# A third panel in flight: four P and PT buffers instead of three, in the attention of a transformer layer

## The chip, the cores and the metric

The kernel runs on the 8 cores of one Trainium2 chip, four on each of its two dies. Every core executes the same program on its own inputs, and no core waits for another. The time is the device time of the slowest core in microseconds, as the median of several runs. The profile is of one execution, read on its slowest core.

## What is computed

One layer on x of 4 sequences x 4096 positions x 2048 features: causal attention with 16 heads of 128, a low-rank key and value path (latent 512), rotary embedding, and then a gated feed-forward with int8 weights (8192 wide), each inside "norm, block, norm, add":

```python
def attn(x):                                  # x is layer-normed
    q = x @ Wq + bq
    kv = x @ Wdown
    k, v = kv @ Wk_up, kv @ Wv_up             # 16 heads of 128
    q, k = rope(q), rope(k)
    scores = einsum('bhqd,bhkd->bhqk', q, k) / sqrt(128)
    scores = where(causal, -10000.0, scores)
    ctx = einsum('bhqk,bhkd->bhqd', softmax(scores), v)
    return ctx @ Wo + bo
def ffn(x):
    return ((silu(x @ w_gate * s_gate) * (x @ w_up * s_up)) @ w_down) * s_down
x = x + layernorm(attn(layernorm(x)))
x = x + layernorm(ffn(layernorm(x)))
```

## The kernel before

Two cores share a sequence. Each computes keys and values for all 4096 positions and takes 16 of the 32 blocks of 128 queries, so chosen that block number tt (0 to 15) of either core sees at most 256 (tt + 1) keys: `wpad(tt)` is that width W.

The program is written as a plan. `plan.step(engine, fn, waits)` appends one step to the list of an engine (T is TensorE, V VectorE, S ScalarE, G GpSimd, Q the SP queue, SyncE), and each engine executes its list strictly in the order of appending. A `Slot` stands for a buffer: `cons_waits` waits for whoever filled it, `prod_waits` also for its last readers. DMAs of one queue share 8 semaphores in turn. There are five stages, A to E, with a barrier over all engines behind each. A makes keys and values, B the queries, C is the attention proper, D the output projection with norm and first sum, E the feed-forward.

Stage C is the one that matters here. It loops over 16 heads h, and within a head over 16 tiles tt. One head and one tile are a panel. For a panel:

- TensorE multiplies the 128 queries with up to 512 keys at a time (L706) into one of four PSUM banks, chunk ci into bank ci. There are 1 to 8 chunks. VectorE adds the causal mask to the last 256 columns (L720) and takes the negated maximum of the first chunk (L728). ScalarE takes the exponential of each chunk with that maximum as bias (L734), writes P in bf16 and accumulates the row sums in `lacc`.
- VectorE adds the row sums (L746) and takes the reciprocal (L750).
- The SP queue issues one DMA transpose of the whole panel from `P_b[par]` to `PT_b[par]` (L756), within SBUF.
- `emit_ctx` multiplies PT with V, W / 128 matmuls of 128 columns (L667), into bank 4 or 5, and VectorE scales the result by the reciprocal into `ctx` (L678).

The context of a panel is not appended in its own iteration. Panels are put in the list `pend`, and `emit_ctx` is called for the oldest when there are more than two. So behind the scores of tile tt stands the context of tile tt - 2, and behind those of tiles 0 and 1 the contexts of tiles 14 and 15 of the head before. On VectorE the eviction of that context stands ahead of the maximum of the next tile. P, PT, `lacc`, `lsum`, `negc` and `rl_s` have three buffers, taken in turn (`par`).

K, V and Q of the next head are loaded by `head_loads(h + 1)` ahead of tile 4: K (L640) and Q (L650) from ScalarE's queue, V as a DMA transpose from HBM (L645) on the SP queue. These have two buffers each. The lines of the core of this:

```python
                pend.append((par, hp, W, tt, h))
                if len(pend) > 2:
                    emit_ctx(pend.pop(0))
        while pend:
            emit_ctx(pend.pop(0))
```

Of the kernel before, what the change touches and what calls it, by code (L numbers as in the profile page):

```python
# [8 lines left out]
BF16 = mybir.dt.bfloat16  # L9
# [120 lines left out]
def build_program():  # L130
# [91 lines left out]
    sg_s = small([64])  # L222
    su_s = small([64])
    st_s = small([16])
    lacc = small([24])
    lsum = small([3])
    negc = small([3])
    rl_s = small([3])
    assert sm_off[0] <= 512

    ps = [e(nc.psum_tensor(f"ps{i}", [128, 512], F32)) for i in range(8)]
# [384 lines left out]
    if "C" in PHASES:  # L616
        ccv = Carver(arena, AR_U)
        k_s = [ccv.take([SEQ], BF16) for _ in range(2)]
        v_t = [ccv.take([32, 128], BF16) for _ in range(2)]
        q_s = [ccv.take([TOK], BF16) for _ in range(2)]  # L620
        P_b = [ccv.take([SEQ], BF16) for _ in range(3)]
        PT_b = [ccv.take([32, 128], BF16) for _ in range(3)]
        mks_s = ccv.take([NH, 256], F32)
        ctx = ar_view(ctxr, 0, [NH, DM], BF16)

        s_k = [Slot(), Slot()]
        s_v = [Slot(), Slot()]
        s_q = [Slot(), Slot()]
        s_P = [Slot(), Slot(), Slot()]
        s_PT = [Slot(), Slot(), Slot()]  # L630
        s_m = Slot()
        s_ctx = Slot()
        s_lac = [Slot(), Slot(), Slot()]
        s_rl = [Slot(), Slot(), Slot()]

        s_m.produced(st("Q", lambda q: q.dma_start(mks_s, mks), dma="dQ"))

        def head_loads(h):
            hp = h % 2
            ev = st("S", lambda s, h=h, hp=hp: s.dma_start(  # L640
                k_s[hp], k_scr[h * 128:(h + 1) * 128, :]),
                waits=prod_waits(s_k[hp]) + cons_waits(scr_slot["k"]),
                dma="dA")
            s_k[hp].produced(ev)
            ev = st("Q", lambda s, h=h, hp=hp: s.dma_start(  # L645
                v_t[hp], v_scr[h * 128:(h + 1) * 128, :], transpose=True),
                waits=prod_waits(s_v[hp]) + cons_waits(scr_slot["v"]),
                dma="dQ", xpose=True)
            s_v[hp].produced(ev)
            ev = st("S", lambda s, h=h, hp=hp: s.dma_start(  # L650
                q_s[hp], q_scr[h * 128:(h + 1) * 128, :]),
                waits=prod_waits(s_q[hp]) + cons_waits(scr_slot["q"]),
                dma="dA")
            s_q[hp].produced(ev)

        head_loads(0)
        pend = []

        def emit_ctx(p):
            (par, hp, W, tt, h) = p  # L660
            cbank = 4 + (len(pend) + h + tt) % 2
            cps, cpa = ps_slot[cbank], ps_ap[cbank]

            def fn(t, par=par, hp=hp, W=W, cpa=cpa):
                r = None
                for kc in range(W // 128):
                    r = t.matmul(cpa[:, 0:128], PT_b[par][:, kc, :],  # L667
                                 v_t[hp][:, kc, :],
                                 start=(kc == 0), stop=(kc == W // 128 - 1))
                return r  # L670
            ev_c = st("T", fn, waits=prod_waits(cps) +
                      cons_waits(s_PT[par], s_v[hp]))
            cps.produced(ev_c)
            s_PT[par].used(ev_c)
            s_v[hp].used(ev_c)

            ev_e = st("V", lambda v, tt=tt, h=h, par=par, cpa=cpa:
                      v.tensor_scalar(ctx[:, tt, h * 128:(h + 1) * 128],  # L678
                                      cpa[:, 0:128],
                                      rl_s[:, par:par + 1], None,  # L680
                                      op0=ALU.mult),
                      waits=cons_waits(cps, s_rl[par]))
            cps.used(ev_e)
            s_rl[par].used(ev_e)
            s_ctx.produced(ev_e)

        pancnt = 0
        for h in range(NH):
            hp = h % 2

            for tt in range(16):
                if tt == 4 and h + 1 < NH:
                    head_loads(h + 1)
                par = pancnt % 3
                pancnt += 1
                W = wpad(tt)
                nch = (W + 511) // 512
                exp_evs = []
                ev_nc = None
                for ci in range(nch):  # L700
                    n0 = ci * 512
                    N = min(512, W - n0)
                    bank = (ci + pancnt * 4) % 4
                    pss, psa = ps_slot[bank], ps_ap[bank]
                    ev_mm = st("T", lambda t, tt=tt, hp=hp, n0=n0, N=N, psa=psa:
                               t.matmul(psa[:, 0:N],  # L706
                                        q_s[hp][:, tt * 128:(tt + 1) * 128],
                                        k_s[hp][:, n0:n0 + N],
                                        start=True, stop=True),
                               waits=prod_waits(pss) +  # L710
                               cons_waits(s_q[hp], s_k[hp]))
                    pss.produced(ev_mm)
                    s_q[hp].used(ev_mm)
                    s_k[hp].used(ev_mm)
                    ev_ready = ev_mm
                    if ci == nch - 1:
                        moff = (W - 256) - n0
                        assert moff >= 0
                        ev_ready = st("V", lambda v, psa=psa, moff=moff, tt=tt:
                                      v.tensor_add(psa[:, moff:moff + 256],  # L720
                                                   psa[:, moff:moff + 256],
                                                   mks_s[:, tt, :]),
                                      waits=[ev_mm] + cons_waits(s_m))
                        pss.produced(ev_ready)
                    if ci == 0:
                        N0 = N
                        ev_nc = st("V", lambda v, psa=psa, N0=N0, par=par:
                                   v.reduce_max(negc[:, par:par + 1],  # L728
                                                psa[:, 0:N0],
                                                axis=AX, negate=True),  # L730
                                   waits=[ev_ready] + prod_waits(s_lac[par]))
                        pss.used(ev_nc)
                    ev = st("S", lambda s, psa=psa, n0=n0, N=N, par=par, ci=ci:
                            s.activation(P_b[par][:, n0:n0 + N], psa[:, 0:N],  # L734
                                         ACT.Exp, bias=negc[:, par:par + 1],
                                         scale=1.0,
                                         accum_out=lacc[:, par * 8 + ci:
                                                        par * 8 + ci + 1]),
                            waits=[ev_ready, ev_nc] +
                            (prod_waits(s_P[par]) if ci == 0 else []))  # L740
                    pss.used(ev)
                    exp_evs.append(ev)
                s_P[par].produced(exp_evs[-1])
                s_lac[par].produced(exp_evs[-1])

                ev_l = st("V", lambda v, par=par, nch=nch: v.reduce_sum(  # L746
                    lsum[:, par:par + 1], lacc[:, par * 8:par * 8 + nch],
                    axis=AX),
                    waits=exp_evs)
                ev_rl = st("V", lambda v, par=par: v.reciprocal(  # L750
                    rl_s[:, par:par + 1], lsum[:, par:par + 1]),
                    waits=[ev_l] + prod_waits(s_rl[par]))
                s_rl[par].produced(ev_rl)
                s_lac[par].used(ev_l)

                ev_t = st("Q", lambda q, par=par, W=W: q.dma_start(  # L756
                    PT_b[par][:, 0:W // 128, :], P_b[par][:, 0:W],
                    transpose=True),
                    waits=cons_waits(s_P[par]) + prod_waits(s_PT[par]),
                    dma="dQ", xpose=True)  # L760
                s_P[par].used(ev_t)
                s_PT[par].produced(ev_t)

                pend.append((par, hp, W, tt, h))
                if len(pend) > 2:
                    emit_ctx(pend.pop(0))

        while pend:
            emit_ctx(pend.pop(0))

        plan.barrier()
# [478 lines left out]
```

How the kernel before makes its waits and increments, by code:

```python
    def replay(self, eng_handle, eng_name, sems):  # L85
        cur = {}
        for ws, fn, sem, inc in self.ops[eng_name]:
            for s, v in ws:
                if cur.get(s, 0) < v:
                    eng_handle.wait_ge(sems[s], v)
                    cur[s] = v
            if fn is None:
                continue
            inst = fn(eng_handle)
            if inc:
                inst.then_inc(sems[sem], inc)
```

## Time and profile before

| | |
|---|---|
| median of 3 runs | 6945.17 us (6869.4 to 7135.95) |
| profiled execution | 6705.15 us |
| its span, slowest core (core 3) | 6703.6 us |
| spans of the 8 cores | 6675.4 to 6703.6 us |
| granted clock, mean of a core | 0.837 to 0.842 |
| busy, share of the span | PE 66%, DVE 25%, ACT 19%, POOL 12% |

The span is from the first to the last instruction of a core. The profiled execution is 1.5 us longer than its span, and 3.5% below the median of the three runs. PE is TensorE (PEld its weight loads), DVE VectorE, ACT ScalarE, POOL GpSimd, SP the queue of SyncE. The granted clock is a share of 2.4 GHz, so 0.50 is the level of 1.2 GHz and 1.00 that of 2.4. In a timeline row stand the start (us from the start of the span), the duration, engine, line, operation, output and input, and in brackets how long the engine sat idle ahead of it and what ended that.

### The profile page before, as it was taken

Reading aid. Unit: us, or ns where it says so; the run is one execution under the profiler, and the core shown is the slowest. Engines: PE = TensorE matmul, PEld = TensorE weight load, DVE = VectorE, ACT = ScalarE, POOL = GpSimd, SP = SyncE. Lnnn points to the kernel's source line nnn. Section 1 sums busy time; section 2 is a strip of 40 time slices with the busy share of each in tenths; the row PEclk is TensorE's granted clock in tenths of the full one; section 3 lists DMA queues with packets and bytes.
Section 4 is the critical chain, followed back from the end, with each engine's and each line's share of the span. In section 5 each row is a group of like instructions: output and inputs, shape, how many; then the busy total and the mean of one; then the engine's idle time right before and its main releaser. Section 6 shows DMA issues by size and latency. Waiting matters only on the chain.

```text
span 6703.6 us, 67697 instructions; the slowest of 8 cores (6675.4 to 6703.6 us)
## 1 busy us (share of the span) xinstructions
PE 4411.7 (66%) x21376; PEld 2030.9 (30%) x21376; DVE 1656.0 (25%) x3157; ACT 1283.3 (19%) x3035; POOL 780.1 (12%) x732
## 2 busy tenths in 40 slices
PE   0334443366566665663333899879998899879986
PEld 0111111133333333341111344334433344334432
DVE  0333433244333333332333111021101211021101
ACT  0111111011555555550111000010000110010100
POOL 0111211133000000000000111111111111111111
PEclk9867776688777777766666999989999999999998
DMA  9333233522777777765443999489967898489954
GB/s 183 96 94 91 75 107 94 129 58 64 140 138 138 139 138 137 138 125 144 129 138 108 165 153 155 128 166 153 151 140 153 152 154 139 128 168 154 153 125 132
DMA packets 1566328, 883.21 MB, mean 132 GB/s; under 512 B 777122, under 2 KB 1541026, under 8 KB 1550242
## 3 DMA queue, kind: packets, MB, share of 16 engines
q0 software_dynamic: 679296, 434.14, 38.0%
q1 hardware_dynamic: 839842, 327.28, 22.0%
q10 hardware_dynamic: 46848, 117.45, 5.2%
q8 instruction: 187, 3.06, 0.2%
q14 instruction: 155, 1.27, 0.1%
HBM read 398.53 MB, written 109.05 MB: 76 GB/s over the span
## 4 chain that ended last, share of the span: by engine, by line
PE 45%; DMA 21%; DVE 11%; ACT 8%; issue 8%; SPq 3%; POOL 2%; another core or an unknown queue 1%; ACTq 0%; DVEq 0%; POOLq 0%
PE ps L994 13%; PE ps L1008 13%; PE ps L1061 7%; DMA arena<-wd 7%; ACT arena L734 5%; PE ps L826 3%; DMA arena<-arena 3%; DMA ctxr<-xin 3%; PE ps L667 2%; PE ps L706 2%; PE ps L395 2%; PE ps L426 2%; POOL arena L589 1%; DMA ctxr<-x_scr 1%; DVE smalls L728 1%
## 5 line engine op out<-in xcount | busy, mean ns | idle before, releaser
L994 PE MATMUL ps<-arena 128*128 128x512 bf16 x4096 | 933.2, 381 | 228.0 <-DMA arena<-x1n_scr 124.4
L1061 PE MATMUL ps<-arena 128*128 128x512 bf16 x4096 | 919.5, 380 | 140.3 <-DMA arena<-wd 138.4
L1008 PE MATMUL ps<-arena 128*128 128x512 bf16 x4096 | 925.8, 379 | 0.6 <-DMA arena<-wu 0.6
L734 ACT ACTIVATE arena<-ps,smalls 128x512 bf16<-128x512 f32 (+1 forms) x1152 | 748.6, 667 | 566.7 <-DVE smalls L728 366.4
L706 PE MATMUL ps<-arena 128*128 128x512 bf16 (+1 forms) x1152 | 473.8, 485 | 376.4 <-ACT arena L734 310.7
L994 PEld LDWEIGHTS ps<-arena 128*128 128x128 bf16 x4096 | 402.1, 98 | 718.5 <-issue 241.4
L395 PE MATMUL ps<-arena 128*128 128x512 bf16 x512 | 128.0, 417 | 722.8 <-DMA arena<-ctxr 722.8
L1061 PEld LDWEIGHTS ps<-arena 128*128 128x128 bf16 x4096 | 385.9, 98 | 673.3 <-issue 245.2
L1024 DVE TENSOR_SCALAR ctxr<-ps,smalls 128x512 bf16<-128x512 f32 x256 | 192.1, 750 | 1450.7 <-PE ps L1008 1450.4
L1008 PEld LDWEIGHTS ps<-arena 128*128 128x128 bf16 x4096 | 400.5, 98 | 484.4 <-issue 1.5
L667 PE MATMUL ps<-arena 128*128 128x128 bf16 x4352 | 417.9, 273 | 170.9 <-DMA arena<-arena 165.1
L984 POOL DMA_DIRECT2D arena<-wg x128 | 146.4, 1143 | 3292.1 <-DMA x1n_scr<-arena 2028.9
L1019 ACT ACTIVATE ctxr<-ps,smalls 128x512 bf16<-128x512 f32 x256 | 175.9, 687 | 1545.3 <-PE ps L994 1543.1
L826 PE MATMUL ps<-arena 128*128 128x512 bf16 x1024 | 229.9, 389 | 333.1 <-DMA arena<-wo_scr 306.1
L667 PEld LDWEIGHTS ps<-arena 128*128 128x128 bf16 x4352 | 376.9, 126 | 231.6 <-issue 223.6
L426 PE MATMUL ps<-arena 128*128 128x512 bf16 x1024 | 295.3, 427 | 121.3 <-DVE arena L461 110.1
L555 PE MATMUL ps<-arena,ctxr 128*128 128x512 bf16 x1024 | 231.0, 390 | 151.2 <-DMA arena<-xnf_scr 151.2
L706 PEld LDWEIGHTS ps<-arena 128*128 128x128 bf16 x1152 | 124.1, 114 | 652.7 <-issue 645.3
L1050 POOL DMA_DIRECT2D arena<-wd x256 | 189.7, 741 | 939.4 <-PE ps L1061 916.1
L395 PEld LDWEIGHTS ps<-arena 128*128 128x128 bf16 x512 | 53.4, 105 | 796.9 <-issue 747.6
L1081 DVE TENSOR_TENSOR ctxr<-ps,ctxr 128x512 f32<-128x512 f32 x64 | 43.9, 691 | 1012.6 <-PE ps L1061 1012.5
L469 POOL TENSOR_TENSOR ctxr<-arena 128x512 bf16<-128x512 f32 x128 | 162.2, 1267 | 946.1 <-DVE arena L461 946.1
(73 smaller groups left out, 2613.6 us busy)
## 6 DMA issues: line engine op xcount, KB each, us to landing
arena<-wg POOLq DMA_DIRECT2D x128, 1024.0 KB, 7.0
arena<-wu POOLq DMA_DIRECT2D x128, 1024.0 KB, 7.1
arena<-wd POOLq DMA_DIRECT2D x256, 512.0 KB, 3.8
ctxr<-xin SPq DMA_DIRECT2D x32, 1024.0 KB, 5.8
arena<-wo_scr ACTq DMA_DIRECT2D x16, 2048.0 KB, 8.9
xnf_scr<-arena SPq DMA_DIRECT2D x16, 1024.0 KB, 7.1
k_scr<-ctxr SPq DMA_DIRECT2D x16, 1024.0 KB, 7.1
v_scr<-ctxr SPq DMA_DIRECT2D x16, 1024.0 KB, 7.8
```

Of the source, the lines that this page charges most:

```text
L395: r = t.matmul(psa, wdn_s[:, fc, lc * 128:(lc + 1) * 128], xnfm[:, fc, :], start=(fc == 0), stop=(fc == NH - 1))
L426: r = t.matmul(psa, wts[:, lc, fc * 128:(fc + 1) * 128], kvl[:, lc, :], start=(lc == 0), stop=(lc == 3))
L555: rr = t.matmul(psa, wq_s[:, fc, oc * 128:(oc + 1) * 128], xnfmB[:, fc, :], start=(fc == 0), stop=(fc == NH - 1))
L667: r = t.matmul(cpa[:, 0:128], PT_b[par][:, kc, :], v_t[hp][:, kc, :], start=(kc == 0), stop=(kc == W // 128 - 1))
L706: t.matmul(psa[:, 0:N], q_s[hp][:, tt * 128:(tt + 1) * 128], k_s[hp][:, n0:n0 + N], start=True, stop=True),
L734: s.activation(P_b[par][:, n0:n0 + N], psa[:, 0:N], ACT.Exp, bias=negc[:, par:par + 1], scale=1.0, accum_out=lacc[:, par * 8 + ci: par * 8 ...
L826: r = t.matmul(psa, ctxfm[tp][:, fc, j * 128:(j + 1) * 128], wo_s[wop][:, fc, :], start=(fc == 0), stop=(fc == NH - 1))
L994: rr = t.matmul(ga, wg_s[slp][:, fc, icw * 128:(icw + 1) * 128], x1nfm[:, fc, :], start=(fc == 0), stop=(fc == NH - 1))
L1008: rr = t.matmul(ua, wu_s[slp][:, fc, icw * 128:(icw + 1) * 128], x1nfm[:, fc, :], start=(fc == 0), stop=(fc == NH - 1))
L1024: ev2 = st("V", lambda v, ic=ic, ua=ua: v.tensor_scalar(u_sb, ua, su_s[:, ic:ic + 1], None, op0=ALU.mult), waits=cons_waits(ub) + prod_wai ...
L1050: return g.dma_start(wd_s[qp], sap)
L1061: rr = t.matmul(psa, f_b[:, quar * 4 + ic, j * 128:(j + 1) * 128], wd_s[qp][:, ic, :], start=(quar == 0 and ic == 0), stop=(quar == 15 and ...
```

## The change

A third panel is in flight. P, PT and the small vectors get a fourth buffer, `emit_ctx` is called when more than three panels are pending, and the loads of the next head stand ahead of tile 5 instead of tile 4.

```diff
-    lacc = small([24])
-    lsum = small([3])
-    negc = small([3])
-    rl_s = small([3])
+    lacc = small([32])
+    lsum = small([4])
+    negc = small([4])
+    rl_s = small([4])
...
-        P_b = [ccv.take([SEQ], BF16) for _ in range(3)]
-        PT_b = [ccv.take([32, 128], BF16) for _ in range(3)]
+        P_b = [ccv.take([SEQ], BF16) for _ in range(4)]
+        PT_b = [ccv.take([32, 128], BF16) for _ in range(4)]
...
-        s_P = [Slot(), Slot(), Slot()]
-        s_PT = [Slot(), Slot(), Slot()]
+        s_P = [Slot() for _ in range(4)]
+        s_PT = [Slot() for _ in range(4)]
...
-        s_lac = [Slot(), Slot(), Slot()]
-        s_rl = [Slot(), Slot(), Slot()]
+        s_lac = [Slot() for _ in range(4)]
+        s_rl = [Slot() for _ in range(4)]
...
-                if tt == 4 and h + 1 < NH:
+                if tt == 5 and h + 1 < NH:
                     head_loads(h + 1)
-                par = pancnt % 3
+                par = pancnt % 4
...
                 pend.append((par, hp, W, tt, h))
-                if len(pend) > 2:
+                if len(pend) > 3:
                     emit_ctx(pend.pop(0))
```

On TensorE, at the boundary from one head to the next, this stands in a row before (L706 are scores, L667 contexts; x30 and x32 are the contexts of tiles 14 and 15, the row of 128x256 alone is tile 0 of the next head):

```order
L667 MATMUL ps5<-arena 128x128 x28
L706 MATMUL ps0<-arena 128x256
L667 MATMUL ps4<-arena 128x128 x30
L706 MATMUL ps0<-arena 128x512
L667 MATMUL ps5<-arena 128x128 x32
L706 MATMUL ps0<-arena 128x512
L706 MATMUL ps1<-arena 128x256
L667 MATMUL ps5<-arena 128x128 x2
```

The context of tile 15 stands behind the scores of tile 1. On the same engine and at the same place it now reads:

```order
L706 MATMUL ps0<-arena 128x256
L667 MATMUL ps4<-arena 128x128 x28
L706 MATMUL ps0<-arena 128x512
L667 MATMUL ps5<-arena 128x128 x30
L706 MATMUL ps0<-arena 128x512
L706 MATMUL ps1<-arena 128x256
L667 MATMUL ps4<-arena 128x128 x32
L706 MATMUL ps0<-arena 128x512
L706 MATMUL ps1<-arena 128x512
L667 MATMUL ps4<-arena 128x128 x2
```

Every context has moved behind the scores of one more tile; that of tile 15 now stands behind those of tile 2. On the SP queue, at the loads of the next head, this is the order (128x8x128 is the transpose of tile 3, 128x10x128 that of tile 4), first before:

```order
L756 DMA_TRANSPOSE arena<-arena 128x8x128
L645 DMA_TRANSPOSE arena<-v_scr 128x32x128
L756 DMA_TRANSPOSE arena<-arena 128x10x128
L756 DMA_TRANSPOSE arena<-arena 128x12x128
```

and after the change:

```order
L756 DMA_TRANSPOSE arena<-arena 128x8x128
L756 DMA_TRANSPOSE arena<-arena 128x10x128
L645 DMA_TRANSPOSE arena<-v_scr 128x32x128
L756 DMA_TRANSPOSE arena<-arena 128x12x128
```

The transpose of V has moved behind the transpose of tile 4. K and Q move by the same tile on ScalarE's queue.

## Rows read from the trace of the kernel before

**Rows 1.** The page: span, and ScalarE's busy tenths in 40 equal slices.
```profile
span 6703.6 us, 67697 instructions; the slowest of 8 cores (6675.4 to 6703.6 us)
...
ACT  0111111011555555550111000010000110010100
```

**Rows 2.** Stretch of stage C: length, busy times, granted clock, DMA share, GB/s.
```profile
1664.00:3030.00 1366.00, 831.70 (x5504) 494.92 (x5504) 424.01 (x1280) 773.16 (x2305) 0.00 (x0) 0.71 0.71 138
```

**Rows 3.** Waits, 1676 to 3030 us: us in total, times, longest.
```profile
ACT arena L734 <- DVE smalls L728: 366.4, 173, 8.9
...
ACT arena L734 <- PE ps L706: 181.7, 79, 4.7
PE ps L667 <- DMA arena<-arena: 165.1, 49, 6.3
...
ACT arena L734 <- PE ps L667: 18.6, 3, 6.4
...
SPq L90 <- ACT arena L734: 495.9, 191, 6.9
```

**Rows 4.** Timeline of ScalarE, head 15: first exponentials of tiles 5 and 8.
```profile
2957.07 0.69 ACT L734 ACTIVATE arena<-ps,smalls 128x512 bf16<-128x512 f32 x1 [1.62 <-DVE smalls L728]
...
2969.41 0.69 ACT L734 ACTIVATE arena<-ps,smalls 128x512 bf16<-128x512 f32 x1 [1.62 <-DVE smalls L728]
```

**Rows 5.** Timeline of ScalarE, tile 2: heads 1 and 15, of 15.
```profile
1768.13 0.69 ACT L734 ACTIVATE arena<-ps,smalls 128x512 bf16<-128x512 f32 x1 [5.89 <-PE ps L667]
...
2947.64 0.69 ACT L734 ACTIVATE arena<-ps,smalls 128x512 bf16<-128x512 f32 x1 [5.47 <-DVE smalls L728]
```

**Rows 6.** Timeline, head 1: tiles 5, 6 and 8, and a context of tile 3.
```profile
1777.57 0.69 ACT L734 ACTIVATE arena<-ps,smalls 128x512 bf16<-128x512 f32 x1 [1.62 <-DVE smalls L728]
...
1780.40 1.01 PE L667 MATMUL ps<-arena 128*128 128x128 bf16 x8 [3.62 <-DMA arena<-arena]
1782.85 0.69 ACT L734 ACTIVATE arena<-ps,smalls 128x512 bf16<-128x512 f32 x1 [3.16 <-PE ps L706]
...
1792.78 0.69 ACT L734 ACTIVATE arena<-ps,smalls 128x512 bf16<-128x512 f32 x1 [1.62 <-DVE smalls L728]
```

**Rows 7.** Timeline from 1923 us: the boundary from head 2 to head 3.
```profile
1923.54 1.83 PE L667 MATMUL ps<-arena 128*128 128x128 bf16 x30
...
1924.19 5.28 SPq L756 DMA_TRANSPOSE arena<-arena  x1
...
1929.22 0.19 ACT L734 ACTIVATION_READ_ACCUMULATOR arena<-ps,smalls 128x1 f32 x1
...
1931.58 3.57 PE L667 MATMUL ps<-arena 128*128 128x128 bf16 x32 [4.58 <-DMA arena<-arena]
...
1936.58 0.69 ACT L734 ACTIVATE arena<-ps,smalls 128x512 bf16<-128x512 f32 x1 [7.17 <-DVE smalls L728]
...
1937.61 0.20 ACT L734 ACTIVATION_READ_ACCUMULATOR arena<-ps,smalls 128x1 f32 x1
...
1939.43 0.69 ACT L734 ACTIVATE arena<-ps,smalls 128x512 bf16<-128x512 f32 x1 [1.62 <-DVE smalls L728]
```

**Rows 8.** Stretches ahead of and behind that wait, columns as in rows 2.
```profile
1920.00:1924.00 4.00, 3.17 (x41) 2.48 (x42) 0.43 (x1) 4.00 (x12) 0.00 (x0) 1.00 0.80 150
...
1932.00:1936.00 4.00, 3.82 (x33) 3.16 (x31) 0.67 (x2) 0.00 (x0) 0.00 (x0) 0.50 0.16 33
```

**Rows 9.** Head 2: load of V, end of tile 4, landings in 1845:1940, then 1863:1868.
```profile
1858.19 7.89 SPq L645 DMA_TRANSPOSE arena<-v_scr  x1
...
1859.88 0.20 ACT L734 ACTIVATION_READ_ACCUMULATOR arena<-ps,smalls 128x1 f32 x1
...
DMA to landing us min/median/max: 2.3/4.5/8.3
...
DMA to landing us min/median/max: 3.6/3.8/4.0
```

**Rows 10.** Stretch behind the loads in head 2, columns as in rows 2.
```profile
1864.00:1868.00 4.00, 2.50 (x12) 1.28 (x12) 1.71 (x5) 0.77 (x3) 0.00 (x0) 0.50 1.27 286
```

## The prediction, made before the result

> **What bounds the kernel now.** I began with the page: the span of the slowest core and the slices in which ScalarE is busy to five tenths [rows 1]. These slices are the attention stage, the only one that the change touches. The stretch query gives its extent, 1664 to 3030 us, 1366 us of 6703.6, with the DMA engines busy to 0.71 and a granted clock of 0.71 on average [rows 2]. Stages end in barriers over all engines, and the cores do not talk to each other, so what this stage loses or gains reaches the end one to one.
>
> Then the waits of this stage [rows 3]. ScalarE sat idle 366.4 + 181.7 + 18.6 = 566.7 us ahead of its exponentials (L734). TensorE waited 165.1 us, in 49 waits, for DMA transposes ahead of the context matmuls (L667). The SP queue, which issues all transposes, waited 495.9 us for ScalarE. No engine is full, so the stage is bound by a chain that goes round once per panel (a panel is one head and one tile of 128 queries, "tile n" below, 256 of them).
>
> The timeline shows that chain. In a quiet panel, ScalarE is idle for 1.62 us between the last exponential of one tile and the first of the next: head 15, which loads nothing, has 1.62 at tiles 5, 6, 7 and 8 [rows 4]. In these 1.62 us VectorE does, in a row, the sum, the reciprocal, the context eviction and the maximum, and ScalarE needs that maximum. 256 x 1.62 = 415 us, which the change leaves alone. So 566.7 - 415 = 152 us is all that ScalarE waits over the bare round, and the most that a perfect pipeline of this form could give back: 2.3% of the span.
>
> Two places hold most of the 152. First, the head boundary. The gap ahead of tile 2 is 5.89 us in head 1 and 5.47 in head 15, the first and the last of 15 such rows, which sum to 99.9 us; less 15 x 1.62 that is 75.6 us [rows 5]. Second, the loads of the next head: ahead of tiles 5 to 7 the gaps of heads 0 to 14 sum to 40.2 us over 1.62 each, 2.7 us per load. In head 1 it is 15.21 us from the start of tile 5 to that of tile 8 (1777.57 to 1792.78), in head 15 it is 12.34 (2957.07 to 2969.41) [rows 4, 6].
>
> **The boundary, step by step** [rows 7]. The transpose of tile 15 of head 2 is issued from 1924.19 on, behind its last exponential, for 5.28 us, and TensorE starts on its context (32 matmuls) at 1931.58, after 4.58 us of idling. Meanwhile tiles 0 and 1 of head 3, one exponential each, are soon done (tile 1 by 1929.41), and tile 2 can't start: its maximum stands on VectorE behind the eviction of this context. The exponential of tile 2 starts at 1936.58, that is 5.00 us after the context began. Tile 3 follows at 1939.43, 2.85 us later.
>
> With a depth of three, the context of tile 15 stands behind the scores of tile 2. What stands ahead of tile 2 is the context of tile 14, whose transpose has long landed: it ran at 1923.54 without a wait. So tile 2 can start at 1929.41 + 1.62 = 1931.0 and, at its 1.23 us (1936.58 to 1937.81), works until 1932.3, while the transpose lands. The context of tile 15 starts at 1931.58 as before, since nothing in the change speeds its transpose. If its matmuls take 3.57 us again, tile 3 starts at 1931.58 + 5.00 = 1936.58 and not at 1939.43: 2.85 us gained, 43 us in 15 boundaries. All 15 gaps are long enough for that: the least is 5.40 us, 3.8 over the 1.62.
>
> How fast these 32 matmuls run sets the rest. The granted clock was 1.00 in 1920 to 1924 and 0.50, the 1.2 GHz level, in 1932 to 1936, after the idling [rows 8]. At the upper level 30 of them took 1.83 us [rows 7], so 32 would take 1.95, and tile 3 could start 1.6 us sooner: 4.5 us per boundary, or, capped where a gap has less than that to give, 64 us in all. TensorE's wait here shrinks from 4.58 us to about 1.3 (from the end of tile 2's scores, near 1930.3), so some boundaries should keep the clock. I take 51, between 43 and 64 and nearer to the row of 3.57. Bounds: 0, if the transpose lands later by as much as is gained, and 75.6, all of it. The Trainium skill (TensorE: Matmul & The Clock Gate, Part 1) calls the half-rate clock the default, which activity releases and idling brings back; by that rule the boundaries would give the 64 us. The trace agrees in so far as the level is the lower one behind the idling and the upper one ahead of it.
>
> Against it: 30 matmuls (tile 14) now stand between the scores of tile 1 and those of tile 2. At the lower level they take some 3.3 us from 1927.0 and end at 1930.3, where the bank is free at 1929.3: 1.0 us late, 15 us in all at worst. It costs nothing as long as tile 3 waits for the context of tile 15 anyway, which it does at the lower level. I take 0 and keep 15 as the bound below nothing.
>
> **The loads.** The load of V is a transpose too, and holds SP for 7.89 us [rows 9]; now it goes ahead of the transpose of tile 4, with K and Q beside it. Therefore the context of tile 3 waits 3.62 us in head 1 [rows 6], and that of tile 4 nearly as long. It moves behind the transpose of tile 4. In head 2, tile 4's transpose would be issued near 1860.2 (its exponentials end at 1860.08), V from about 1861.5 to 1869.4, tile 5's transpose at 1869.4, landed by 1873.4 (4.0 us, the longer of two there [rows 9]). The context of tile 5 is now due behind the scores of tile 8, not before 1875: in time by 1.6 us. That of tile 4, if its landing is as slow as the slowest in that head, 8.3 us [rows 9], lands at 1868.5 and is due at 1870. A further 2 us would be hidden, since a wait of 3.62 us on TensorE cost ScalarE only 3.16 - 1.62 = 1.54 [rows 6]. I take 38 of the 40.2 us; bounds 0 and 40.2. What hides it is the third panel in flight. Without that, moving the load by a tile would only move the wait, and the 38 us would be 0.
>
> The Trainium skill (Perfetto Trace Analysis, What "DMA-bound" means) names as a bound an issuing engine whose sequencer track is solid with DMA work. More buffers would then give nothing, which is the second rival below. Here SP waited for ScalarE for 495.9 of 1354 us [rows 3], so its track isn't solid.
>
> **The rest** costs nothing: the fourth P and PT buffer only follow the depth, and no wait of before is for one of them to come free; the drain behind the last head still waits for the transpose of its tile 15; the start of the stage is the same; instructions and bytes are the same in number.
>
> **The sum.** 51 + 38 = 89 us. The profiled execution took 6705.15 us around a span of 6703.6, so its like would take 6616, 1.3% less. The runs shown have a median of 6945.17 and a lowest of 6869.4, both well above the profiled one. The stage's waits are counted in absolute microseconds, so I take the same 89 off the median: 6856 us.
>
> **Rivals.**
> *The loads' waits only move.* T4's landing or V's hold on SP is longer beside wider transposes, and contexts 5 and 6 wait at tiles 8 and 9 instead. The DMA engines were full (a share of 1.27 from 1864 to 1868) behind the loads in head 2 [rows 10], and the margin is only 1.6 us; but 2 us more are hidden. Then 51 us is gained: 6894.
> *Nothing is gained.* SP or the DMA engines bind, and tile 15's transpose lands as much later as its context is due later. 495.9 us of SP's waiting speaks against. 6945.
> *Nearly all goes.* The clock stays high through the boundaries, and the smaller gaps (152 - 116 = 36 us) shrink, since each tile has two context matmuls fewer beside it. Then 130 to 150 us: 6805, and past 2% at the far end.
> *Slower.* The loads now meet the transposes of tiles 4 to 6, wider than 3 to 5, and the big contexts of tile 14 delay the scores of tile 2 at the lower clock. If the load's waits double (40 us more) and the boundary gives nothing but pays its 15 us, 55 us are lost: 7000. It decides when TensorE's waits for transposes rise above 165.1 us; nothing in the rows of before points there.
>
> **How the numbers follow.** The forecast has 0.65, moved waits 0.14, nothing 0.06, nearly all 0.10, slower 0.05. All cases together reach from 6805 to 7000, and the runs of before alone lie 1.1% below to 2.7% above their median, which the median of a few new runs inherits in part; so 6710 to 7000. 2% of the median, 139 us, is about what a measurement of this kernel can tell from no change. Only the far end of one case is beyond it by itself; with the spread of runs I give 0.18 to faster by over 2%, 0.78 to within 2%, and 0.04 to slower.
>
> **What would show it.** In the profile after: the stage some 89 us shorter than 1366; TensorE's wait for transposes ahead of L667 down from 165.1 us to under 40; the gap ahead of tile 2 near 1.6 to 2.6 us, and one of 2 to 4 us ahead of tile 3 in its place; tiles 6 and 7 at 1.62 as in head 15; everything outside the stage as before. Waits for transposes that appear ahead of tiles 8 and 9 would show the moved wait. The forecast is wrong if the gap ahead of tile 2 stays above 5 us, or if the gap at tile 3 takes its whole length.

## The result, and the profile after

| | before | after |
|---|---|---|
| median of 10 runs | 6891.2 us | 6692.67 us |
| lowest run | 6707.85 us | 6604.59 us |
| ratio, with 95% interval | | 0.9845 (0.9829 to 0.9861) |
| first to last exponential of stage C, mean of cores 4 to 7 | 1333.7 us | 1232.2 us |
| the same, mean of all 8 cores, after in the second measurement | 1333.9 us | 1234.1 us |

About half of the runs of either kernel were disturbed, with a lower clock on one die or both, and the three runs of before that were known ahead were all of that kind: the ratio is taken without such runs, while the medians hold both. The ratio is a gain of 1.55%, 104 us of the 6705 of the profiled execution (0.0155 x 6705). In a second measurement, with runs of the kernel before beside it, the ratio was 0.9863 (0.982 to 0.9905). The forecast was 89 us, 1.3%.

"The stage" is here the time from the first exponential of stage C to the last. In the trace of the first measurement cores 4 to 7 had nearly the same granted clock as before (0.841 to 0.844, against 0.839 to 0.842), and they are the ones read. There the stage of core 4 took 1333.6 us before and 1228.8 after (1686.9 to 2915.7), 105 us less; the mean of the four cores fell by 101.5 us, and in the second measurement the mean of all eight by 99.8. The profiled core of before, core 3, is the longest of its eight with 1337.7 us (1678.8 to 3016.6), so it can't be set against another core. The rest of the span of cores 4 to 7 was 9 us longer on average, 5363.9 us against 5354.8. The change does not touch it, and it differs by as much and more between single executions, as the part on depth alone shows.

The rows below are of the changed kernel in the second measurement, core 3, whose stage took 1237.9 us. First the page, and the stretch of the stage with the columns of [rows 2]:

```profile
span 6614.1 us, 67712 instructions; the slowest of 8 cores (6580.0 to 6614.1 us)
...
ACT  0111111111566666641111000010000100010000
```

```profile
1664.00:2930.00 1266.00, 837.78 (x5495) 481.47 (x5496) 415.04 (x1279) 772.21 (x2305) 0.00 (x0) 0.70 0.77 149
```

ScalarE's busy time is the same, 772 us against 773, in 100 us less. The DMA share rose from 0.71 to 0.77, the same transfers in a shorter stage. The waits of the stage, which answer to [rows 3]:

```profile
ACT arena L734 <- DVE smalls L728: 354.0, 195, 5.3
ACT arena L734 <- PE ps L706: 86.5, 47, 2.2
...
ACT arena L734 <- PE ps L667: 24.8, 12, 4.0
PE ps L667 <- DMA arena<-arena: 24.6, 16, 3.1
ACT arena L734 <- DVE ps L720: 2.5, 1, 2.5
...
SPq L90 <- ACT arena L734: 378.7, 176, 5.2
```

TensorE waits 24.6 us for transposes where it waited 165.1. ScalarE idles 354.0 + 86.5 + 24.8 + 2.5 = 467.8 us where it idled 566.7: 98.9 us less, and the stage of this core is 99.8 us shorter. So ScalarE's gaps account for all that the stage gained. The boundary from head 1 to head 2, in the timeline, which answers to [rows 7]:

```profile
1834.62 1.84 PE L667 MATMUL ps<-arena 128*128 128x128 bf16 x30
...
1836.37 0.69 ACT L734 ACTIVATE arena<-ps,smalls 128x512 bf16<-128x512 f32 x1 [2.28 <-DVE smalls L728]
...
1837.29 0.48 PE L706 MATMUL ps<-arena 128*128 128x512 bf16 x2 [0.83 <-ACT arena L734]
...
1838.24 1.95 PE L667 MATMUL ps<-arena 128*128 128x128 bf16 x32 [0.47 <-DMA arena<-arena]
...
1838.76 0.69 ACT L734 ACTIVATE arena<-ps,smalls 128x512 bf16<-128x512 f32 x1 [1.62 <-DVE smalls L728]
...
1841.61 0.69 ACT L734 ACTIVATE arena<-ps,smalls 128x512 bf16<-128x512 f32 x1 [1.62 <-PE ps L667]
```

The x32 row is the context of tile 15. It stands behind the scores of tile 2 (the row of 1837.29), waits 0.47 us and takes 1.95. Tile 2 (1838.76) starts after 1.62 us, tile 3 (1841.61) too. Not every boundary goes so well. The next one, and the stretches that hold the two contexts:

```profile
1916.85 3.57 PE L667 MATMUL ps<-arena 128*128 128x128 bf16 x32 [2.38 <-DMA arena<-arena]
...
1921.86 0.69 ACT L734 ACTIVATE arena<-ps,smalls 128x512 bf16<-128x512 f32 x1 [5.16 <-DVE smalls L728]
```

```profile
1836.00:1840.00 4.00, 2.70 (x43) 2.20 (x41) 1.71 (x6) 2.01 (x6) 0.00 (x0) 1.00 0.63 124
...
1916.00:1920.00 4.00, 3.15 (x30) 3.18 (x31) 0.32 (x2) 0.69 (x4) 0.00 (x0) 0.50 0.41 82
```

At the granted clock of 1.00 the 32 matmuls take 1.95 us, at 0.50 they take 3.57, and then tile 3 waits 5.16 us. On this core 9 of the 15 contexts took 1.95 us, on core 4 of the first measurement 13 of 15; on core 3 of the kernel before none took less than 2.81. The idle time just ahead does not decide it alone: on this core one context took 1.95 us behind 2.11 us of idling, and another 3.55 us behind 1.36. Ahead of tile 2 all gaps but one are 1.62 us, and those ahead of tile 3 sum to 21.2 us over 15 x 1.62 here, the most of the eight cores, whose mean is 16.6; on core 4 of the first measurement it is 12.0. And the tiles 6, 7 and 8 of head 2, where [rows 6] shows 3.16 ahead of tile 6:

```profile
1852.30 0.69 ACT L734 ACTIVATE arena<-ps,smalls 128x512 bf16<-128x512 f32 x1 [1.62 <-DVE smalls L728]
1856.49 0.69 ACT L734 ACTIVATE arena<-ps,smalls 128x512 bf16<-128x512 f32 x1 [1.62 <-DVE smalls L728]
1860.89 0.69 ACT L734 ACTIVATE arena<-ps,smalls 128x512 bf16<-128x512 f32 x1 [1.62 <-DVE smalls L728]
```

The sum of the parts, in gaps of ScalarE over 1.62 us, as the mean of the eight cores, before and then here: ahead of tiles 2 and 3 together 70.3 and 16.9 us, so the boundaries gave 53; ahead of tiles 5 to 8, where the loads were felt, 42.1 and 0.9, so 41; in the smaller gaps 36.1 and 30.8, so 5. That is 99.9 us. The boundary gap of core 3 before, 75.6 us, was the largest of the eight, and the others had 68.4 to 70.6. On the same core the boundaries gave 54 us (core 3) and, in the first measurement, 56 (core 4).

### The profile page after: what moved, and what is told of

The parts are those of the page before. It is cut to its first block, busy times and chain, and to the rows that moved or that the text cites. A ratio compares the mean times of both kernels' runs of the same rounds, so it can differ in the third digit from the quotient of the medians.

```text
span 7057.4 us, 67712 instructions; the slowest of 8 cores (6587.7 to 7057.4 us)
## 1 busy us (share of the span) xinstructions
PE 4964.1 (70%) x21376; PEld 2139.6 (30%) x21376; DVE 1647.3 (23%) x3157; ACT 1282.5 (18%) x3035; POOL 782.1 (11%) x732
## 4 chain that ended last, share of the span: by engine, by line
PE 49%; DMA 17%; DVE 11%; ACT 9%; issue 8%; POOL 2%; SPq 2%; another core or an unknown queue 1%; ACTq 0%; DVEq 0%; POOLq 0%
PE ps L994 15%; PE ps L1008 15%; PE ps L1061 10%; ACT arena L734 6%; DMA arena<-wd 6%; DMA ctxr<-xin 3%; PE ps L826 3%; PE ps L395 2%; PE ps L426 2%; DMA arena<-arena 2%; DVE smalls L728 2%; PE ps L706 2%; POOL arena L589 1%; DMA ctxr<-x_scr 1%; PE ps L667 1%
## 5 line engine op out<-in xcount | busy, mean ns | idle before, releaser
L994 PE MATMUL ps<-arena 128*128 128x512 bf16 x4096 | 1120.7, 437 | 218.1 <-DMA arena<-x1n_scr 122.9
L1061 PE MATMUL ps<-arena 128*128 128x512 bf16 x4096 | 1101.6, 435 | 48.8 <-DMA arena<-wd 45.4
L1008 PE MATMUL ps<-arena 128*128 128x512 bf16 x4096 | 1114.9, 435 | 0.0
L706 PE MATMUL ps<-arena 128*128 128x512 bf16 (+1 forms) x1152 | 486.1, 485 | 404.8 <-ACT arena L734 331.7
L994 PEld LDWEIGHTS ps<-arena 128*128 128x128 bf16 x4096 | 445.2, 109 | 850.5 <-issue 838.3
L1061 PEld LDWEIGHTS ps<-arena 128*128 128x128 bf16 x4096 | 426.7, 107 | 723.0 <-issue 711.0
L395 PE MATMUL ps<-arena 128*128 128x512 bf16 x512 | 129.1, 419 | 728.1 <-DMA arena<-ctxr 728.1
L1008 PEld LDWEIGHTS ps<-arena 128*128 128x128 bf16 x4096 | 444.3, 108 | 626.0 <-issue 612.9
L826 PE MATMUL ps<-arena 128*128 128x512 bf16 x1024 | 228.7, 387 | 327.4 <-DMA arena<-wo_scr 299.9
L667 PE MATMUL ps<-arena 128*128 128x128 bf16 x4352 | 401.3, 266 | 39.5 <-DMA arena<-arena 31.5
L667 PEld LDWEIGHTS ps<-arena 128*128 128x128 bf16 x4352 | 362.6, 122 | 87.3 <-issue 76.5
L426 PE MATMUL ps<-arena 128*128 128x512 bf16 x1024 | 295.5, 428 | 123.7 <-DVE arena L461 112.7
L706 PEld LDWEIGHTS ps<-arena 128*128 128x128 bf16 x1152 | 117.9, 109 | 714.1 <-issue 708.4
L395 PEld LDWEIGHTS ps<-arena 128*128 128x128 bf16 x512 | 53.6, 106 | 803.1 <-issue 754.6
```

The source lines that it names most:

```text
L395: r = t.matmul(psa, wdn_s[:, fc, lc * 128:(lc + 1) * 128], xnfm[:, fc, :], start=(fc == 0), stop=(fc == NH - 1))
L426: r = t.matmul(psa, wts[:, lc, fc * 128:(fc + 1) * 128], kvl[:, lc, :], start=(lc == 0), stop=(lc == 3))
L667: r = t.matmul(cpa[:, 0:128], PT_b[par][:, kc, :], v_t[hp][:, kc, :], start=(kc == 0), stop=(kc == W // 128 - 1))
L706: t.matmul(psa[:, 0:N], q_s[hp][:, tt * 128:(tt + 1) * 128], k_s[hp][:, n0:n0 + N], start=True, stop=True),
L826: r = t.matmul(psa, ctxfm[tp][:, fc, j * 128:(j + 1) * 128], wo_s[wop][:, fc, :], start=(fc == 0), stop=(fc == NH - 1))
L994: rr = t.matmul(ga, wg_s[slp][:, fc, icw * 128:(icw + 1) * 128], x1nfm[:, fc, :], start=(fc == 0), stop=(fc == NH - 1))
```

## The experiments

### Depth alone

The changed kernel with the loads left ahead of tile 4:

```diff
-                if tt == 5 and h + 1 < NH:
+                if tt == 4 and h + 1 < NH:
```

Expected, of the first run:

> The third panel in flight with its four buffers, the loads left ahead of tile 4. My theory is that the depth hides both waits and that the place of the loads matters little: the context of tile 3 is due behind the scores of tile 6 and that of tile 4 behind those of tile 7, some 4 us later than before, and the waits were 2.5 to 4.6 us. Then tiles 6 and 7 start after 1.62 us and the whole takes about 6605 us, within 10 us of the changed kernel. The rival, that moving the loads cured their part, expects the 40 us to stay: gaps of 2.4 and 3.1 us ahead of tiles 6 and 7, or the same ahead of 7 and 8, and about 6645 us.

and of a second with more rounds, beside the changed kernel itself, whose expectation stands here too:

> The same kernel as depth_only, timed in more rounds. Its trace had all gaps ahead of tiles 5 to 8 at 1.62 us, so the theory that depth does both parts expects 0.984 to 0.987 of before. The rival, that the place of the loads gives a gain that the gaps don't show, expects a difference of over 15 us to the changed kernel.

> The changed kernel itself, on the chip on which the next three run, so that they can be compared with it. Theory: 0.984 to 0.985 of before; the stage 105 to 110 us shorter, TensorE's waits for transposes near 26 us, of which all but a few are at the head boundaries.

Measured: the lowest run was 6634.81 us in the first and 6630.07 in the second, where the changed kernel had 6615.64 and before 6726.87. Neither has a ratio. The trace of the second is clearer. Its wait of TensorE for transposes, and ScalarE at tiles 6 and 7 of head 2:

```profile
PE ps L667 <- DMA arena<-arena: 46.0, 31, 2.9
```

```profile
1893.03 0.69 ACT L734 ACTIVATE arena<-ps,smalls 128x512 bf16<-128x512 f32 x1 [1.62 <-DVE smalls L728]
...
1897.22 0.69 ACT L734 ACTIVATE arena<-ps,smalls 128x512 bf16<-128x512 f32 x1 [1.62 <-DVE smalls L728]
```

On this core all gaps ahead of tiles 6 and 7 are 1.62 us but one of 1.97. The waits of 46.0 us, against 24.6 in the changed kernel, are longer by those of the contexts of tile 4 (23.6 us in 15 waits, where the changed kernel has none), and nearly none of it reached ScalarE: the stage took 1234.4 us as the mean of the eight cores, against 1234.1. So the depth does both parts, and the place of the loads gives nothing in the stage. The 14 us between the lowest runs don't come from there either. The profiled executions are 24 us apart (6639.7 and 6615.64 us), and in them the depth alone begins stage C later on every core, by 26 us on average. So that difference stands in stages A and B, where the two kernels have the same steps. What makes it is open.

### The place of the loads alone

The kernel before, with `tt == 4` made `tt == 5` and nothing else:

> Two panels in flight and three buffers as before, only the loads of the next head moved ahead of tile 5. My theory expects the waits to move by one tile: contexts of tiles 4 and 5 wait, the gaps of 2.5 and 3.1 us stand ahead of tiles 7 and 8, the boundary is as before with 6.3 us ahead of tile 2, and the time is that of before within 15 us, 6705. The rival, that the place of the loads is what gains, expects 6665 us with 1.62 us ahead of tiles 6 to 8.

> The same kernel as loads_only, timed in more rounds. Its trace showed the waits moved from tiles 6 and 7 to tiles 7 and 8, with 29 us over the 1.62 where before had 40, so 0.997 to 1.001 of before. The rival that the move gains by itself would need 0.994 or less.

Measured in the second, with more rounds: 0.9989 (0.9973 to 1.0005), no difference of note. The first had a lowest run of 6725.75 us and no ratio. The timeline of head 2, ScalarE at tiles 6, 7 and 8, and TensorE:

```profile
1882.12 0.69 ACT L734 ACTIVATE arena<-ps,smalls 128x512 bf16<-128x512 f32 x1 [1.62 <-DVE smalls L728]
1887.24 0.69 ACT L734 ACTIVATE arena<-ps,smalls 128x512 bf16<-128x512 f32 x1 [2.54 <-PE ps L706]
1892.65 0.69 ACT L734 ACTIVATE arena<-ps,smalls 128x512 bf16<-128x512 f32 x1 [2.62 <-PE ps L706]
```

```profile
1884.58 1.23 PE L667 MATMUL ps<-arena 128*128 128x128 bf16 x10 [3.03 <-DMA arena<-arena]
...
1890.26 0.96 PE L667 MATMUL ps<-arena 128*128 128x128 bf16 x12 [2.75 <-DMA arena<-arena]
```

The waits are those of contexts 4 (x10) and 5 (x12) instead of 3 and 4, ahead of tiles 7 and 8 instead of 6 and 7. The move by itself moves the wait, as expected. A part of it goes all the same: as the mean of the eight cores the gaps ahead of tiles 5 to 8 are 33.2 us over 1.62 where before had 42.1, and the stage took 1325.3 us against 1333.9, each in one execution. That is 0.13% of the span, which the interval of the ratio holds.

### The clock at the boundary

The kernel before, with matmuls that fill TensorE's wait. Their result is read by nobody, and nothing of the computation changes:

```diff
                 if len(pend) > 2:
+                    if tt == 1 and h > 0:
+                        def fnk(t, hp=hp):
+                            r = None
+                            for _ in range(46):
+                                r = t.matmul(ps_ap[6][:, 0:128],
+                                             q_s[hp][:, 0:128],
+                                             k_s[hp][:, 0:128],
+                                             start=True, stop=True)
+                            return r
+                        ev_k = st("T", fnk, waits=prod_waits(ps_slot[6]) +
+                                  cons_waits(s_q[hp], s_k[hp]))
+                        ps_slot[6].produced(ev_k)
+                        s_q[hp].used(ev_k)
+                        s_k[hp].used(ev_k)
                     emit_ctx(pend.pop(0))
```

> The kernel before, with 46 extra matmuls of 128 columns, into a bank that nobody reads, ahead of the context of tile 15 at each head boundary, where TensorE was idle for 3.4 to 6.3 us. They fill about 2.8 us of that wait at the upper clock. If the granted clock is what made the 32 matmuls take 3.57 us, they now take 1.95, the gap ahead of tile 2 falls by up to 1.6 us from 6.6, and the kernel gains 15 to 24 us: 6685. If something else sets their duration (their operands just landed by DMA), they stay near 3.3 to 3.57 us and the time at 6705.

Measured: 0.9983 (0.9932 to 1.0034), which tells nothing about 15 to 24 us. The trace does. TensorE on core 0 (its granted clock is 0.844, and 0.840 in the kernel before), at the boundary to head 2 (L770 is the filling), and the stretch that holds the context:

```profile
1837.17 2.73 PE L770 MATMUL ps<-arena 128*128 128x128 bf16 x46 [1.52 <-DVE smalls L746]
1841.46 1.95 PE L667 MATMUL ps<-arena 128*128 128x128 bf16 x32 [1.55 <-DMA arena<-arena]
```

```profile
1840.00:1844.00 4.00, 2.22 (x33) 1.91 (x34) 0.66 (x4) 0.00 (x0) 0.00 (x0) 1.00 0.41 81
```

The context took 1.95 us at 11 of 15 boundaries of this core, where it took 2.46 to 3.57 on the same core of before. Ten gaps ahead of tile 2 fell below 5.7 us, eight of them to 4.92 or less, while five stayed between 6.39 and 7.54. The mean of the 15 went from 6.26 (before, same core) to 5.64: 9 us in all, and the mean stage of cores 0 to 3 went from 1334.1 to 1325.1 us, 9 us too, below the expected 15 to 24. The operands still land just ahead of the context, which waits 1.55 us for them, and yet it takes 1.95 us at a granted clock of 1.00. So the clock, not the operands that just landed, sets the duration, and matmuls in the wait kept the clock at most boundaries.

### One panel more

The changed kernel with five buffers and `if len(pend) > 4`:

> Four panels in flight and five buffers, loads ahead of tile 5. My theory: with three in flight the context of tile 15 still waits, 0.5 to 2.9 us, and tile 3 starts 0.8 us late on average (12 us in all). With four it is due behind the scores of tile 3 and finds its transpose landed: tile 3 at 1.62 us, TensorE's waits for transposes down from 26 us to the 3 to 5 of the drain, and 8 to 12 us less than the changed kernel, about 6595. The rival, that more depth brings nothing further, expects the time of the changed kernel within 4 us, 6605.

> The same kernel as depth4, timed in more rounds. Its trace had the last excess ahead of tile 3 gone, some 12 to 20 us less idling of ScalarE than the changed kernel, so 0.981 to 0.983 of before. The rival, no further gain, expects 0.984 to 0.985.

Measured, in the second: 0.9823 (0.9795 to 0.9852), beside 0.9863 (0.982 to 0.9905) of the changed kernel on the same chip. The intervals overlap. In the trace of the first, on core 3 (granted clock 0.837), the gaps ahead of tile 3 are at 1.62 us but for two (1.90 and 1.81), no wait of TensorE for a transpose is left, and the stage took 1214.4 us. Two rows of TensorE and ScalarE there: the context of tile 15 without a wait, and the tile after it:

```profile
1869.44 1.95 PE L667 MATMUL ps<-arena 128*128 128x128 bf16 x32
1870.59 0.69 ACT L734 ACTIVATE arena<-ps,smalls 128x512 bf16<-128x512 f32 x1 [1.62 <-DVE smalls L728]
```

I expected 8 to 12 us over the changed kernel. The stage gives twice that: as the mean of the eight cores in the second, 1234.1 - 1213.7 = 20.4 us, of which 16 stood ahead of tile 3 and 5 in smaller gaps. The 12 us behind my figure were those of one core with few slow contexts.

### The chain itself

What remains is the gap of 1.62 us or a little more ahead of nearly every tile. This version puts the first scores and the maximum of the next panel ahead of the sum, the reciprocal and the eviction of this one (and on TensorE ahead of the context), and lets the chunks go round six banks. The steps of a panel, cut to what is new (`first_chunk` appends scores, mask and maximum of chunk 0 just as the loop did, `score` those of any chunk):

```diff
+        SBK = (0, 1, 2, 3, 6, 7)
...
+        fc = first_chunk(0)
...
-                    bank = (ci + pancnt * 4) % 4
...
+                    if ci == 0:
+                        bank, ev_ready, ev_nc = fc
+                    else:
+                        bank, ev_ready = score(tt, hp, ci, W)
...
                 s_lac[par].produced(exp_evs[-1])
+                if pancnt < NH * 16:
+                    fc = first_chunk(pancnt)

                 ev_l = st("V", lambda v, par=par, nch=nch: v.reduce_sum(
```

> The changed kernel, with the first scores and the maximum of the next panel put ahead of the row sum, reciprocal and context eviction of this one (and on TensorE ahead of the context), and score chunks going round six PSUM banks instead of four. My theory is that the 1.62 us ahead of every tile, 415 us in all, are a chain through VectorE and not the work of any engine. Then ScalarE goes from tile to tile in under 0.5 us where a tile has several chunks, until the next bound: the SP queue was issuing in 874 of the changed kernel's 1255 us and ScalarE was busy in 771, so the stage should take 950 to 1100 us and the kernel 6300 to 6450. The rival, that the transposes bind as soon as ScalarE is faster, expects TensorE's waits for transposes to grow from 26 us to over 150 and a time of 6500 or more.

Measured: 0.9476 (0.9435 to 0.9517), runs of 6369 to 6395 us. The stage took 983.4 us on the profiled core, 975.7 as the mean of the eight. Its stretch, and its waits (L760 is the exponential there, L701 the scores, L715 the mask, L774 the row sum):

```profile
1707.00:2692.00 985.00, 657.97 (x5408) 399.79 (x5408) 414.21 (x1271) 765.03 (x2305) 0.00 (x0) 0.86 1.02 185
```

```profile
PE ps L667 <- DMA arena<-arena: 160.0, 59, 5.6
...
ACT arena L760 <- DMA arena<-arena: 78.8, 39, 4.0
ACT arena L760 <- DVE ps L715: 64.0, 30, 3.8
ACT arena L760 <- DVE smalls L774: 34.5, 34, 2.1
ACT arena L760 <- PE ps L701: 31.0, 34, 1.4
...
SPq L90 <- ACT arena L760: 65.4, 73, 4.2
```

ScalarE idles some 220 us instead of 468, and the wait for the maximum (L728 in the changed kernel) is gone. The DMA engines are now at a share of 1.02 in the stage, the SP queue waits for ScalarE only 65.4 us, and TensorE waits 160 us for transposes again. ScalarE itself waits 78.8 us for transposes, those that must have read a P buffer before it is written again. Half of the rival came true: TensorE's waits rose above its 150 us and the transposes are the largest wait now, but the time stayed over 100 us below its 6500. The Trainium skill (Perfetto Trace Analysis, What "DMA-bound" means) names a solid track of the issuing engine as one bound: here it is nearly that, where before it waited 495.9 us. Which of the two binds, SP's issuing or the DMA engines, no run here separates. A part of the gain may be TensorE's: its granted clock in the stage is 0.86 where the changed kernel has 0.70, and it is busy for 658 us instead of 838. No run separates that from the new order, which it came with.

Two parts of it by themselves:

> The changed kernel with only the score chunks going round six PSUM banks instead of four. If the chain through VectorE sets the pace, the gap of 1.62 us stays and the time is within 15 us of the changed kernel, 6605, at best with the 1.85 ahead of tiles 9 and 10 brought to 1.62. If the banks set it (TensorE waits 324 us for ScalarE ahead of the scores), the kernel gains 50 us or more: 6550.

> As early_max, but with four PSUM banks. The first scores of the next tile then need bank 0, which the exponential of chunk 0 or 4 of this tile frees: late in tiles of one or five chunks, early in those of three, four, seven and eight. My theory expects gaps of 1.2 to 1.5 us to stay ahead of tiles that follow one or five chunks, and small ones elsewhere, so roughly two thirds of what early_max gains: 6400 to 6500. The rival, that TensorE's own order is the limit (the context now stands behind first scores that wait for a bank), expects less than 50 us: 6555 or more.

Six banks alone: a lowest run of 6629.06 us, no ratio, and no gain over the changed kernel's 6604.59 to 6616. ScalarE's wait for the maximum stayed, while TensorE waited four times as long for transposes as in the changed kernel:

```profile
ACT arena L736 <- DVE smalls L730: 405.6, 236, 4.2
...
PE ps L667 <- DMA arena<-arena: 97.1, 40, 5.1
```

The stage is as long as the changed kernel's, 1232.3 us against 1234.1 as the mean of the eight cores, but two things cancel. The smaller gaps shrank from 30.8 to 13.5 us (those ahead of tiles 9 and 10 fell from 1.85 to 1.62, as expected), and the gaps ahead of tile 3 grew from 16.6 to 32.0 us over 1.62. There the context of tile 15 waited 3.2 to 5.1 us and took 2.34 to 3.57 us at the 13 boundaries whose rows stand by themselves, so none of them ran at the upper clock throughout.

The early maximum with four banks: runs of 6405.75 and 6494.73 us. The lower one is within 40 us of early_max, and the stage in the trace of the upper one is 988.2 us as the mean of the eight cores, against 975.7 of early_max and 1234.1 of the changed kernel. So the new order gives 246 of the 258 us, far more than the two thirds that I expected.

> As early_max, with four panels in flight and five buffers. If early_max still waits for transposes at the head boundary, because the faster ScalarE reaches the context of tile 15 sooner while its transpose takes as long, this takes these waits away and gains 20 to 60 us over early_max. If the throughput of the SP queue or of the DMA engines is the bound, more depth moves nothing: within 10 us of early_max.

Measured: 0.9422 (0.9381 to 0.9462), 6335 to 6361 us, about 36 us below early_max (0.0054 x 6705). The intervals overlap, but the stage is 941.1 us as the mean of the eight cores, 35 less than in early_max, about half of it ahead of tile 3 and half ahead of tiles 5 to 8. So the first branch of the expectation held: in early_max a part of the waits for transposes was the time until one lands, which more depth hides, and not the throughput of SP or the DMA engines alone. What is left may be SP's: in the chain of work that ended last, its issuing of the panels' transposes (L784) has 25.9% of the stage here, on core 0, and 5.4% in early_max, on core 3. It is the fastest of all that ran. The DMA share in the stage was 1.05.

## Why the prediction was right or wrong

**The mechanism held.** The context of tile 15 waits behind the scores of tile 2, tile 2 starts after 1.62 us, and what is left is ahead of tile 3. The loads' waits are gone. Depth alone shows that the third panel hides them, and the loads alone that the move by a tile mostly moves them, as the step on the loads said. The drain did not change.

**The boundary's term** was 51 us, between 43 at the lower clock and 64 at the upper. It gave 53 as the mean of the eight cores, 54 and 56 on the two cores read against themselves. So it was right to 3 us on the core that it was worked out for. Its two prices hold as well: with 9 of 15 boundaries at the upper clock they make 43 + 9/15 x 21 = 56 us there. What was a little too low is the share of boundaries that keep the clock, which 51 us puts at 6 in 15. Filling the wait in the kernel before showed that the clock is what sets the context's duration. The Trainium skill (TensorE: Matmul & The Clock Gate, Part 1) says that activity releases the lower clock and idling brings it back, and by that rule I had put the boundaries at 64 us. The traces agree in that the upper level was kept more often where TensorE idled less, but 6 of 15 boundaries of core 3 lost it all the same, and 54 us came out.

**The loads' term** was 38 us and gave 39 on this core, 41 as the mean of the eight. The margins that I worked out, 1.6 us and 2 us hidden, sufficed. That they were tight is seen in depth alone: 21 us more waiting on TensorE, nearly none of it on ScalarE.

**The sum** was 89 us, and the stage gave 99.9 us (mean of the eight cores): 2 us more at the boundaries, 3 at the loads, and 5 in small gaps, which the sum had at nothing. As a ratio, 1.3% was forecast and 1.55% measured.

**The level failed.** The step "I take the same 89 off the median: 6856 us", with the range "6710 to 7000" built on it, rests on a median of three runs, all of them above the profiled execution by 2.4% or more. I noted that and kept the median; and for the lower end I let the best case, 6805 us, fall by only 1.4%, as if these three runs spanned what a run can be. With seven more runs, four of the kernel before took 6707.85 to 6717.22 us. Of the changed kernel's ten runs five took 6604.59 to 6613.01 us and five 6772.32 to 7164.79, and the median of 6692.67 is the mean of 6613.01 and 6772.32, a time near which no run lay. It is 17 us under the range's lower end. It was not the gain that put it there: with the measured ratio in place of the 89 us, the same step gives 0.9845 x 6945.17 = 6838 us, off by 145. And it was in part chance: had six of the ten runs been of the upper kind, the median would have lain at 6772 us or more, within the range. The medians of before and after differ by 198.5 us, of which the ratio gives the change 104. The profiled execution at 6705 was a run too: less 89, it gives 6616, and five runs of the changed kernel came within 12 us of that. A range that took it as its lower case would have gone down to 6600.

**The rivals.** Moved waits: not in the changed kernel, but the loads alone show most of them. Nothing is gained: false; SP's waiting for ScalarE fell from 495.9 to 378.7 us and left room. Nearly all goes: the boundaries gave 53 of 70 us and the small gaps 5 of 36. Slower: TensorE's waits for transposes fell to 24.6 us, far from its point of decision.

## What to carry to other kernels

One more panel in flight pays where an engine waits for a transfer and other panels could be worked on meanwhile. Count the gaps over the bare round first, since that sum (152 us here) is the ceiling, and price what is left of a wait by the clock that it leaves behind. Where nearly the same gap stands ahead of every tile, as here where 201 of the 256 gaps before were 1.6 to 2.2 us, look for a chain through an engine's order: three, four and five buffers left the 1.62 us as they were, while putting the one value that the next tile needs ahead of this tile's bookkeeping, with six banks, gained another 3.9% over the changed kernel (0.9476 / 0.9863), over twice what the third panel did. Compare a stage on the same core, or as the mean of all: one core's boundary gaps were 5 us and more above those of every other. And when the runs known lie well above the profiled execution, both levels belong in the range.

## What the runs showed that I had not expected

ScalarE's recorded durations grew once it had no gaps, and it was not slower. Two exponentials and the reads between them, from the timeline of early_max:

```profile
2002.42 0.91 ACT L760 ACTIVATE arena<-ps,smalls 128x512 bf16<-128x512 f32 x1
2002.99 0.42 ACT L760 ACTIVATION_READ_ACCUMULATOR arena<-ps,smalls 128x1 f32 x1
2003.08 0.91 ACT L760 ACTIVATE arena<-ps,smalls 128x512 bf16<-128x512 f32 x1
2003.65 0.43 ACT L760 ACTIVATION_READ_ACCUMULATOR arena<-ps,smalls 128x1 f32 x1
```

The durations are 0.91 us where the kernel before has 0.69, but the starts are 0.66 us apart here and 0.68 there (1936.58 and 1937.26 for two exponentials of a tile). Records overlap, so a pace is read from starts and not from durations.

TensorE's waits for transposes are a poor measure of loss by themselves: 24.6, 46.0 and 97 us of them on the profiled cores of the changed kernel, depth alone and six banks, with stages of 1238, 1234 and 1231 us. It matters where they stand. Those at the loads (21 us in depth alone) reached ScalarE in nearly nothing, and those at the boundaries in six banks cost 15 us ahead of tile 3, which smaller gaps elsewhere gave back.
